# Four stacked graph layers on one core: A0 made ahead of W3's split, late weights asked for later, and half-width spare products in all idle places of TensorE

## What is computed

```
# layer 0: e = (x W1)(x W2)^T, leaky relu, adjacency mask, softmax over nodes; relu(att @ (x W3))
# layer 1: graph attention, h = x W, e_ij = leaky(h_i a1 + h_j a2), mask, softmax, elu(att @ h)
# layer 2: relu MLP to 512, unmasked attention, elu + residual, MLP to 256, masked attention, elu + residual, relu
# layer 3: four-head masked attention with q, k, v and an output projection
x = layernorm(x + L0(x, adj, W1, W2, W3))
x = layernorm(x + L1(x, adj, W, a))
x = layernorm(x + L2(x, adj, mlp1, ..., W_hand, a_hand))
x = layernorm(x + L3(x, adj, wq, bq, wk, bk, wv, bv, wo, bo))
```

## Time and profile before

| what | us |
|---|---|
| median of 3 runs (2617.55 to 2623.7) | 2618.84 |
| the profiled execution, its time | 2616.98 |
| the profiled execution, its span | 2615.2 |
| TensorE busy (PE) | 2525.4 |
| VectorE busy (DVE) | 2251.1 |
| ScalarE busy (ACT) | 1968.4 |
| GpSimd busy (POOL) | 1913.2 |

### The profile page before, as it was taken

How to read it: one execution, slowest core, us unless ns; L and a number is a source line. 1 busy time by engine, 2 the same in 40 slices (tenths; PEclk the granted TensorE clock), 3 DMA queues, 4 the chain that set the end, 5 groups by cost and what they waited for, 6 DMA issues and landing times. The chain is left out here.

```text
span 2615.2 us, 64667 instructions
## 1 busy us (share of the span) xinstructions
PE 2525.4 (97%) x21399; PEld 2411.0 (92%) x21399; DVE 2251.1 (86%) x6252; ACT 1968.4 (75%) x4737; POOL 1913.2 (73%) x2439
## 2 busy tenths in 40 slices
PE   6899999999999999999999999999999999999886
PEld 5789999999999999999999999999999999999874
DVE  2478999899999998999999999999989999998874
ACT  2468877887887788778778877877887788787652
POOL 2457877877787877778787777878777787877543
PEclk8899999999999999999999999999999999999998
DMA  4214444444444444444444444344444444443333
GB/s 141 67 52 128 129 142 130 126 139 130 136 123 145 127 126 142 129 138 121 145 126 130 139 134 133 124 142 128 131 134 136 132 128 141 128 132 110 105 106 89
DMA packets 317115, 329.67 MB, mean 126 GB/s; under 512 B 35313, under 2 KB 248689, under 8 KB 316785
## 3 DMA queue, kind: packets, MB, share of 16 engines
q1 hardware_dynamic: 316784, 325.54, 41.5%
HBM read 174.41 MB, written 150.99 MB: 124 GB/s over the span
## 5 line engine op out<-in xcount | busy, mean ns | idle before, releaser
L1234 POOL TENSOR_TENSOR p<-p,rd 128x512 f32<-128x512 f32 x256 | 343.1, 1350 | 5.5
L1159 POOL TENSOR_TENSOR proT_lo<-sco,proT_hi 128x512 fp32r<-128x512 f32 x128 | 165.8, 1295 | 159.7 <-ACT proT_hi L560 159.7
L1171 POOL TENSOR_SCALAR xn<-act,nmean,rstd 128x256 f32<-128x256 f32 x384 | 237.1, 627 | 47.7 <-DVE act L1075 35.3
L786 ACT ACTIVATE p<-p,nmx 128x256 f32<-128x256 f32 x512 | 253.0, 496 | 10.9 <-DVE nmx L1109 10.9
L573 ACT ACTIVATE sco<-sco,nmax 128x256 f32<-128x256 f32 x384 | 192.6, 502 | 40.9 <-DVE nmax L872 36.1
L1181 POOL TENSOR_TENSOR act<-act,x 128x512 f32<-128x512 f32 x64 | 82.9, 1295 | 167.8 <-ACT act L623 167.8
L1109 DVE CUSTOM_DVE_ANT_0 p<-ps,mask 128x256 f32<-128x256 f32 x512 | 188.3, 414 | 15.4 <-PE ps L510 14.0
L872 DVE CUSTOM_DVE_ANT_0 sco<-ps,mask 128x256 f32<-128x256 f32 x384 | 144.9, 414 | 53.2 <-ACT ps L563 41.2
L808 DVE TENSOR_TENSOR xnT_lo<-ps,xnT_hi 128x512 fp32r<-128x512 f32 x192 | 129.7, 675 | 61.0 <-ACT xnT_hi L560 61.0
L1166 POOL TENSOR_TENSOR rstd<-vare,mhalf 128x2 f32<-128x2 f32 x256 | 178.1, 696 | 0.0
L1124 DVE STREAM_TRANSPOSE p<-p 128x1024 f32<-128x1024 f32 x128 | 158.6, 1239 | 18.0 <-POOL p L1234 17.7
(11 more groups left out here) (240 smaller groups left out, 12396.6 us busy)
## 6 DMA issues: line engine op xcount, KB each, us to landing
scratch<-p SPq DMA_DIRECT2D x128, 512.0 KB, 3.0
p4T<-scratch SPq DMA_DIRECT2D x512, 128.0 KB, 3.5
scratch_pro<-act SPq DMA_DIRECT2D x192, 256.0 KB, 2.3
sco<-scratch_pro SPq DMA_DIRECT2D x768, 64.0 KB, 1.9
x0Tp<-in_xT SPq DMA_DIRECT2D x64, 256.0 KB, 2.6
x<-in_x SPq DMA_DIRECT2D x64, 256.0 KB, 2.8
scratch_o<-sco SPq DMA_DIRECT2D x64, 256.0 KB, 2.1
o3r<-scratch_o SPq DMA_DIRECT2D x256, 64.0 KB, 2.5
```

The source lines that it names most:

```text
L786: ins = nc.scalar.activation(rows_, rows_, ACT.Exp, scale=-1.0, bias=nmx4[:, h, m:m + 1], accum_out=den4[:, h, m:m + 1])
L1159: return G.tensor_tensor(lo, whole, hi.bitcast(fp32), ALU.subtract)
L1171: ins = G.tensor_scalar(xn[:, m, :], y[:, m, :], nmean[i][:, m:m + 1], rstd[i][:, m:m + 1], ALU.add, ALU.mult)
L1234: G.tensor_tensor(rows_, rows_, rd4[:, h, :].unsqueeze(2).unsqueeze(3).broadcast_to([P, NT, QUADS, CT * QP]), ALU.mult).then_inc(S["p4n"], 1)
```

## The change

It has four parts. The three `SPARE` tables name nearly the same places with three to four and a half times the counts (95 becomes 373, 52 becomes 185, 188 becomes 694; one place is new, ahead of m3 of the third last sample). A spare product is now `ones2` times `ones2`, with 128 moving columns in place of 256, made by a helper `busy`; 100 of them stand ahead of the wait for the first weights and 24 between A0's product and its use. GpSimd fills `ones2` at the start. W3 and adj get a semaphore of their own and are asked for behind the first `xT`; VectorE makes A0 first, then W3's parts, then the mask, and TensorE waits for W3's parts ahead of h0. Layer 3's weights are asked for behind the second sample's `xT`.

```diff
-SPARE_OPENING = "h0:0:4 s0:0:3 g0:1:17 a0:0:7 h0:1:4 s0:1:4 x0:0:4 h1:0:15 h0:2:3 s0:2:3 x0:1:4 h0:3:3 s0:3:3 m2:0:16 a1:1:5"
+SPARE_LOADING = 100
+SPARE_OPENING = "h0:0:18 s0:0:18 g0:1:57 a0:0:25 h0:1:18 s0:1:16 x0:0:18 h1:0:46 h0:2:14 s0:2:16 x0:1:18 h0:3:14 s0:3:16 m2:0:52 a1:1:27"
...
-        LOADS = (("W1T", "W2T", "W3"), ("W_T", "a1", "W_"), ...
-        n_loads = [len(LOADS[0]) + 1, ...
+        LOADS = (("W1T", "W2T"), ("W_T", "a1", "W_"), ...
+        n_loads = [len(LOADS[0]), ...
...
             def later_weights():
-                sp.dma_start(adj_sb, adj).then_inc(S["loaded0"], 16)
+                sp.dma_start(W["W3"], weights["W3"]).then_inc(S["loaded4"], 16)
+                sp.dma_start(adj_sb, adj).then_inc(S["loaded4"], 16)
...
-                load_weights(3)
...
                 if t == 0:
                     later_weights()
+                if t == 1:
+                    load_weights(3)
...
+            def busy(b, count):
+                for _ in range(count):
+                    nc.tensor.matmul(ps[:, b, 0:P], ones2[:, :], ones2[:, :], start=True, stop=True)
+
+            pe.wait_ge(S["setup_pool"], 2)
+            busy(4, SPARE_LOADING)
             pe.wait_ge(S["loaded0"], 16 * n_loads[0])
...
             ins.then_inc(S["setup_pe"], 1)
+            busy(4, 24)
             pe.wait_ge(S["made"], 1)
...
-                b, count = spare.get((name, t), (0, 0))
-                for _ in range(count):
-                    nc.tensor.matmul(ps[:, b, 0:N], WP["W3"][0][:, 0, 0:P], WP["W3"][0][:, 1, :], start=True, stop=True)
+                busy(*spare.get((name, t), (0, 0)))
...
-            dv.wait_ge(S["loaded0"], 16 * n_loads[0])
-            V.tensor_scalar(mask16[:, :, :], adj_sb, 0.0, MASK, ALU.is_le, ALU.mult)
-            split([whole_weight("W3")])
             dv.wait_ge(S["setup_pe"], 1)
             V.tensor_copy(A0f[:, :, :], bank[0]).then_inc(S["setup_dve"], 1)
             dv.wait_ge(S["setup_dve"], 1)
             split([(A0, slice(0, CT), slice(0, C), A0f[:, :, :])]).then_inc(S["made"], 1)
+            dv.wait_ge(S["loaded4"], 32)
+            split([whole_weight("W3")]).then_inc(S["made"], 1)
+            V.tensor_scalar(mask16[:, :, :], adj_sb, 0.0, MASK, ALU.is_le, ALU.mult)
...
             def made_fc():
-                dv.wait_ge(S["setup_pool"], 1)
                 dv.wait_ge(S["setup_pe"], 3)
-                V.tensor_copy(ones2[:, :], ones[:, 0:1].broadcast_to([P, P]))
...
             G.memset(ones[:, :], 1.0).then_inc(S["setup_pool"], 1)
-            po.wait_ge(S["setup_pool"], 1)
+            G.memset(ones2[:, :].bitcast(fp32), 1.0).then_inc(S["setup_pool"], 1)
+            po.wait_ge(S["setup_pool"], 2)
```

More of the change, by code:

```diff
@@ L14 @@
 }
-SPARE_OPENING = "h0:0:4 s0:0:3 g0:1:17 a0:0:7 h0:1:4 s0:1:4 x0:0:4 h1:0:15 h0:2:3 s0:2:3 x0:1:4 h0:3:3 s0:3:3 m2:0:16 a1:1:5"
-SPARE_FILLING = "r2:0:5 s0:4:3 m2:1:2 d2:0:11 m2:2:2 f3:0:29"
-SPARE_CLOSING = "m3:-5:2 x1:-3:2 a3:-5:2 m3:-4:2 x1:-2:2 a3:-4:11 x1:-1:2 r2:-1:6 m3:-2:7 s40:-3:3 a3:-2:17 m3:-1:17 s40:-2:3 s42:-2:5 a3:-1:19 a4:-2:25 s40:-1:1 s42:-1:5 a4:-1:52 y4:-1:5"
+SPARE_LOADING = 100
+SPARE_OPENING = "h0:0:18 s0:0:18 g0:1:57 a0:0:25 h0:1:18 s0:1:16 x0:0:18 h1:0:46 h0:2:14 s0:2:16 x0:1:18 h0:3:14 s0:3:16 m2:0:52 a1:1:27"
+SPARE_FILLING = "r2:0:20 s0:4:16 m2:1:11 d2:0:37 m2:2:11 f3:0:90"
+SPARE_CLOSING = "m3:-5:12 x1:-3:11 a3:-5:29 m3:-4:12 x1:-2:11 a3:-4:38 m3:-3:12 x1:-1:11 r2:-1:24 m3:-2:26 s40:-3:15 a3:-2:55 m3:-1:61 s40:-2:15 s42:-2:20 a3:-1:49 a4:-2:88 s40:-1:11 s42:-1:20 a4:-1:154 y4:-1:20"
 def spare_products(B):
@@ L174, in graph_stack @@
         bank = [ps[:, b, :].rearrange("p (m n) -> p m n", m=2) for b in range(8)]
-        names = """loaded0 loaded1 loaded2 loaded3 made wsplit setup_pe setup_dve setup_pool
+        names = """loaded0 loaded1 loaded2 loaded3 loaded4 made wsplit setup_pe setup_dve setup_pool
  x0T_in x0_in x0Th x0Tl g0_mm g0h g0 h0_mm h0h h0 s0_mm raw0 nmax0 pro0 rden0 pro0_x pro0_dma proT0h proT0 av0_mm act0 y0 mv0 rstd0
@@ L208, in graph_stack @@
         scratch_o3 = nc.dram_tensor("scratch_o3", [P, QUADS, CT * N // QUADS], fp32, kind="Internal").ap()
-        LOADS = (("W1T", "W2T", "W3"), ("W_T", "a1", "W_"), ("mlp1", "b1", "afc", "mlp2", "b2", "hand", "hand_T", "ahand", "m1"), ("wqT", "bq", "wkT", "bk", "wvT", "bv", "woT", "bo"))
-        n_loads = [len(LOADS[0]) + 1, len(LOADS[1]) + 1, len(LOADS[2]) + 2 + HT, len(LOADS[3])]
+        LOADS = (("W1T", "W2T"), ("W_T", "a1", "W_"), ("mlp1", "b1", "afc", "mlp2", "b2", "hand", "hand_T", "ahand", "m1"), ("wqT", "bq", "wkT", "bk", "wvT", "bv", "woT", "bo"))
+        n_loads = [len(LOADS[0]), len(LOADS[1]) + 1, len(LOADS[2]) + 2 + HT, len(LOADS[3])]
         @block.sync
@@ L338, in mixed_columns @@
                 pe.wait_ge(S["loaded2"], 16 * n_loads[2])
-                pe.wait_ge(S["setup_pool"], 1)
+                pe.wait_ge(S["setup_pool"], 2)
                 for m in range(CT):
@@ L547, in keep_busy @@
             def keep_busy(name, t):
-                b, count = spare.get((name, t), (0, 0))
-                for _ in range(count):
-                    nc.tensor.matmul(ps[:, b, 0:N], WP["W3"][0][:, 0, 0:P], WP["W3"][0][:, 1, :], start=True, stop=True)
+                busy(*spare.get((name, t), (0, 0)))
             run("pe", {"g0": g0, "h0": h0_, "s0": s0, "a0": a0, "x0": x0_, "h1": h1_, "f1": f1, "a1": a1, "x1": x1_, "m2": m2, "n2": n2, "c2": c2, "r2": r2, "f2": f2, "d2": d2, "v2": v2, "w2": w2,
                        "m3": m3, "h3": h3_, "f3": f3, "a3": a3, "x3": x3_, "q4": q4, "k4": k4, "v4": v4_, "s40": s40, "s42": s42, "a4": a4, "y4": y4}, B,
-                {"a0": graph_columns, "h1": made(2), "a1": mixed_columns, "m2": made(3), "n2": made(3), "c2": made(4), "m3": made(5), "q4": made(6), "k4": made(6), "v4": made(6)}, keep_busy)
+                {"h0": made(2), "a0": graph_columns, "h1": made(3), "a1": mixed_columns, "m2": made(4), "n2": made(4), "c2": made(5), "m3": made(6), "q4": made(7), "k4": made(7), "v4": made(7)}, keep_busy)
         @block.scalar
```

## The result

The changed kernel takes 2646.95 us (median of 5 runs, 2643.88 to 2648.66), the kernel before beside it 2617.55 (5 runs, 2615.26 to 2623.7): ratio 1.0108, 95% interval 1.0093 to 1.0123. It is slower by some 29 us; 2645 were predicted.

The account below looks back on a forecast made before the run. TensorE, issuing practically back to back in the middle, was taken to bound the kernel, so changes at its ends move the end: 2617.0 + 19.7 (opening) + 8.5 (closing) = 2645 us; this case alone 2630 to 2662, overall range 2601 to 2662.

Parts of the forecast that it names:

- The price: Spare products of 128 columns: 0.112 us at the high clock, 0.213 at the low; half the width saves nearly nothing.
- Rival C: Short products of this type are slower, 0.213 us at the high clock: above 2800 us; chance 5%.
- Loading: Start: 100 products at 0.213 us don't raise the clock, end at 22.4; g0 starts 14.9 us later.
- D: Start: the early A0 doesn't happen, loading products swallow the 3.6 us freed; in all sums above 2605, no own chance.
- Asked for later: SP's queue: eight transfers behind the second xT delay scratch_pro and a0's wait, 0 to 3 us, taken as 1.5.
- clock in the opening: Opening: six low stretches go, 10.1 us back; a low stretch from two-column products costs 4.7; net -5.4 us.
- Groups: Opening: 21 groups, 558 products, 62.5 us, reach 10.1 us beyond their places; 1.4 goes into a0's wait.
- Closing: Closing: 694 products reach 15.3 us beyond their places; clock gives back 3.8, waits about 3; +8.5 us.
- Rivals A and B: Spare product price: A, half (0.06 and 0.11), 2605 us, 18%; B, in between (0.083 and 0.16), 2617, 12%.

Follow-up runs that it names:

- e3_wide: Spare products with 256 moving columns instead of 128, against the changed kernel: 2643.11 us.
- e6_bf16: Spare products of the same width on a bf16 tile of ones, against the changed kernel: 2620.23 us.
- e1_noload: The loading products cut from 100 to 0, against the changed kernel: 2629.43 us.
- e4_dma_back: Layer 3's eight weight transfers back at the end of the first queue, against the changed kernel: 2639.11 us.
- e7_best: Changed kernel with 256-column spare products, counts fitted to places, 14 loading, 14 behind A0's product, layer 3's weights behind first sample's scratch_pro reads: 2608.28 us.

## Why the prediction was right

By its own steps, with the measured value:

| step | predicted | measured |
|---|---|---|
| spare product, high and low clock | 0.112, 0.213 | 0.111 (57 in 6.31), 0.213 |
| passes for A0 | 22.4 | 22.46 |
| g0 | +14.9 | +14.8 |
| groups, late transfers and clock behind g0 | +4.8 | +9.6 |
| closing | +8.5 | +6.5 |
| middle | 0 | -0.9 |
| sum | +28.2 | +29.9 |

**The price** of a half-width product was the step that decided, and it was right. Of its reason, that the weight load sets the pace, e3_wide shows that the moving columns don't (twice as many cost almost nothing), and e6_bf16 that the 4-byte type does (bf16 costs half); between the weights' load and another cost of that type no run decides. Rival C falls with them.

**Loading** was right in size, and the clock did not rise. The reason for that holds only in part. One of its two rows was a stretch at 0.50 with products twice as wide, and e3_wide shows that such products back to back do raise the clock, from 6.6 us on. So that row could not carry the "no", and luck had a part in it. In the changed kernel the clock rose only during A0's passes, after 21.4 us of narrow products: the first passes start 0.43 us apart, and the 24 products behind them take 2.8 us. e1_noload returns 17.5 for the loading; D, that the early A0 is swallowed, is shown too: without the loading products g0 comes 3.0 ahead of the kernel before, with them 14.8 behind.

**Asked for later** was undersized: 1.5, within 0 to 3. I counted the issues (1 us; it was 1.43) and left the bytes in between mostly uncounted: 1.3 MB ahead in the same queue made the landing 2.6 us later. Of 4.0 us, 3.5 reached a0, and behind its wait came a low stretch worth 6.8, which the sum had at 4.7 and put down to the two-column products. e4_dma_back has those products too, 8 ahead of a0, and no low stretch there; so the term **clock in the opening** named the wrong cause. Those products alone do not bring it; what e4_dma_back takes away is 3.5 us of the wait ahead of a0. 7.8 us of the total hang on eight transfers that the prediction had at 1.5.

**Groups**: the opening's 558 products took 65.3 us against 62.5 predicted; 34 of them at 1.2 GHz are 3.4 us more. The 1.4 that a0's wait was to absorb was not absorbed, since that wait grew. **Closing**: the groups grew by 16.6 (61.1 to 77.7), as predicted with the new one (15.3 and 1.3); waits and clock gave back 10.2, where the sum had 8.1 (6.8, and 1.3 for the new group). The two errors, +4.8 and -2.0, partly cancel, and the middle, put at nothing, took off another 0.9: the total was closer than its terms.

**Rivals A and B** were ways the price could have gone. e6_bf16 is A's world, at 0.056 and 0.107, and it gave 2620.23, not 2605: A left out the late transfers and the idle part of each place, and 3.1 us of the middle have no explanation. Had A come true, its time would have been missed by 15 us.

What stays open: why the 100 half-width products leave the clock at 1.2 GHz and the same number in bf16 or at full width don't. e3_wide varies only their width and e6_bf16 only their type, and either is enough; the reason is not shown. Nor was it tried how much of e7_best's gain each of its edits carries.

## What to carry to other kernels

Price a filler instruction from the nearest row before multiplying it by a count: halving the moving columns of a 4-byte product saved 7% here (0.12 to 0.112). Filler is worth only the idle time that it covers, so fit each count to the length of its place, put none in front of work that could start, and don't read a busy share of 99% as success. When transfers are moved in a queue, look at the next latency-bound transfer behind their new place, and count bytes as well as issues: the wait can cost again through the clock.

## What the runs showed of the hardware

- A stream of weight load and product at 128 x 128 with 128 moving columns: 0.112 us at 2.4 GHz in float32r, 0.056 in bf16; at 1.2 GHz 0.213 and 0.107. With 256 columns in float32r 0.12 and 0.213.
- From the start of the program, 100 products back to back: float32r with 128 columns all at the low pace (21.4 us), float32r with 256 in 14.5, bf16 with 128 in 7.0 (8.18 less 1.21). The profile prints PEclk 1.00 there in all three; only the spacing tells.
- A 256 KB transfer issued behind eight others (1.3 MB) of the same queue was read 4.58 us after its issue, without them 2.01. The Trainium skill ("DMA: Bandwidth & Descriptors", Queues, rings and completion order) says that each DMA engine takes a queue's descriptors in ring order; the two rows agree.
